# A third of the pair products with samples on partitions, summed along the free axis on ScalarE

## The reference

```python
e = jnp.stack([tbl_0[ids[:, 0]], ..., tbl_39[ids[:, 39]]], axis=1)
vi = x[:, i_idx, :]
vj = x[:, j_idx, :]
viW = jnp.einsum('bpd,pde->bpe', vi, W)
out = jnp.einsum('bpe,bpe->bp', viW, vj)
...
h = jnp.concatenate([z, dense_ctx], axis=1)
h = jnp.maximum(h @ W_top1 + b_top1, 0.0)
h = jnp.maximum(h @ W_top2 + b_top2, 0.0)
y = h @ W_top3
```

## Time and profile before

| | before |
|---|---|
| median of three runs | 1374.25 us |
| the profiled execution's own time | 1374.48 us |
| its span, first to last instruction | 1372.7 us |
| TensorE busy | 1307.9 us, 95% |
| VectorE busy | 928.9 us, 68% |
| GpSimd busy | 604.8 us, 44% |
| ScalarE busy | 83.4 us, 6% |
| mean granted TensorE clock | 0.994 |

### The profile page before, as it was taken

How to read it: one execution, slowest core, us unless ns; L and a number is a source line. 1 busy time by engine, 2 the same in 40 slices (tenths; PEclk the granted TensorE clock), 3 DMA queues, 4 the chain that set the end, 5 groups by cost and what they waited for, 6 DMA issues and landing times.

```text
span 1372.7 us, 17118 instructions
## 1 busy us (share of the span) xinstructions
PE 1307.9 (95%) x7024; PEld 463.4 (34%) x7024; DVE 928.9 (68%) x804; ACT 83.4 (6%) x137; POOL 604.8 (44%) x646
## 2 busy tenths in 40 slices
PE   0699999998999999999999999999999999999998
PEld 0233333332333333333333333333333333333333
DVE  0378877776634788788854588878873478888860
ACT  0000000000000000000000100000000000000001
POOL 6777777777777777754543444451000000000000
PEclk9899999999999999999999999999999999999999
DMA  4233332222222233322211222222110011111100
GB/s 163 42 73 73 70 69 73 73 66 65 65 42 58 66 74 72 74 66 63 65 45 37 47 66 62 62 64 53 47 40 23 23 48 51 50 47 47 32 1 0
DMA packets 49782, 77.38 MB, mean 56 GB/s; under 512 B 13540, under 2 KB 13540, under 8 KB 49576
## 3 DMA queue, kind: packets, MB, share of 16 engines
q1 hardware_dynamic: 29216, 55.26, 13.6%
q0 software_dynamic: 20480, 21.01, 8.4%
q10 hardware_dynamic: 8, 0.01, 0.0%
HBM read 76.22 MB, written 0.01 MB: 56 GB/s over the span
## 4 chain that ended last, share of the span: by engine, by line
PE 86%; POOL 9%; issue 3%; DMA 1%; ACT 1%; POOLq 0%
PE u_ps L311 48%; PE z_ps L328 25%; POOL rows L268 9%; PE turn_ps L342 6%; PE turn_ps L294 3%; PE turn_ps L347 2%; PE u_ps L342 1%; PE u_ps L313 1%; PE u_ps L347 1%; PE turn_ps L351 0%; DMA rows<-in_tbl,ids_all 0%; ACT h_sb L418 0%; DMA ids_all<-in_ids 0%; PE u_ps L351 0%; ACT y_row L424 0%
## 5 line engine op out<-in xcount | busy, mean ns | idle before, releaser
L388 DVE TENSOR_TENSOR prod<-u_ps,x 128x1024 f32<-128x1024 f32 x800 | 928.2, 1218 | 401.8 <-PE u_ps L313 398.4
L313 PE MATMUL u_ps<-x,w_ring 64*128 64x512 f32 x1600 | 759.9, 610 | 0.0
L311 PE MATMUL u_ps<-x,w_ring 64*128 64x512 f32 x1600 | 759.9, 610 | 0.0
L268 POOL DMA_INDIRECT rows<-in_tbl,ids_all x640 | 604.1, 944 | 326.9 <-issue 196.1
L311 PEld LDWEIGHTS u_ps<-x,w_ring 64*128 64x128 f32 x1600 | 279.9, 187 | 420.4 <-issue 324.9
L328 PE MATMUL z_ps<-prod,ones 128*32 128x512 f32 x3200 | 393.4, 601 | 0.0
L313 PEld LDWEIGHTS u_ps<-x,w_ring 64*128 64x128 f32 x1600 | 279.8, 187 | 0.0
L328 PEld LDWEIGHTS z_ps<-prod,ones 128*32 128x32 f32 x3200 | 85.6, 109 | 279.7 <-issue 152.4
L294 PE MATMUL turn_ps<-ident,rows 128*128 128x128 f32 x320 | 53.9, 293 | 60.3 <-DMA rows<-in_tbl,ids_all 54.3
L407 ACT COPY x<-turn_ps 128x512 f32<-128x512 f32 x80 | 46.9, 586 | 635.8 <-PE turn_ps L294 635.8
L342 PE MATMUL turn_ps<-z_sb,mlp_sb 128*128 128x512 f32 x182 | 81.5, 599 | 0.8 <-ACT z_sb L412 0.8
(11 more groups left out here) (19 smaller groups left out, 14.7 us busy)
## 6 DMA issues: line engine op xcount, KB each, us to landing
w_ring<-in_w_pair SPq DMA_DIRECT2D x200, 256.0 KB, 2.7
rows<-in_tbl,ids_all POOLq DMA_INDIRECT x640, 2.5
mlp_sb<-in_mlp SPq DMA_DIRECT2D x1, 2308.0 KB, 11.5
ids_all<-in_ids SPq DMA_DIRECT2D x1, 320.0 KB, 3.3
z_sb<-in_dense_t SPq DMA_DIRECT2D x4, 32.0 KB
out_y<-y_row ACTq DMA_DIRECT2D x4, 2.0 KB
```

Of the source, the lines that this page charges most:

```text
L268: nc.gpsimd.indirect_dma_start(rows[:, slot, s, par * DIM:(par + 1) * DIM], None, tables[f], bass.IndirectOffsetOnAxis(ap=ids_all[:, SUB * ...
L311: pe.matmul(u_ps[:, bank, :], w_ring[0:DIM, c % W_SLOTS, cols], x[0:DIM, b % 2, n_even, :], start=True, stop=True)
L313: pe.matmul(u_ps[:, bank + 1, :], w_ring[DIM:P, c % W_SLOTS, cols], x[DIM:P, b % 2, n, :], start=True, stop=True).then_inc(mains_done, 1)
L388: nc.vector.tensor_tensor(prod[:, full % PROD_SLOTS], u_ps[:, bank:bank + 2, :], other, ALU.mult).then_inc(prods_done, 1)
```

## The change

256 of the 780 pairs are computed the other way round. These are the pairs of duos 4 to 19 with the first four duos (`KEEP`), 64 full units of each block. In their place come 64 units of a new kind, `"R"`: (n, s) is duo n with 128 samples, number s of the block's four. The stationary operand is now 128 samples of the duo (64 partitions), and the matrices of eight pairs move, 512 columns. The product has samples on partitions and eight pairs of 64 numbers along the free axis. VectorE multiplies it with the gathered rows of the first four duos as they came, which are now held for a block in `kept`, and writes one of four slots of `rprod`. The sum over d then runs along the free axis: on ScalarE by 16 instructions of 128x64 with an accumulator output, or, for the first 24 of the new units (all in the first block), on VectorE by one `tensor_reduce`. The sums collect in `zb`, samples on partitions; two turns by TensorE per block (`"zr"`) bring them into two chunks of `z_sb`. The others fill five chunks, so the first dense layer has seven as before.

The units of both kinds are interleaved by `block_units`. The number of slots of `rows` falls from 10 to 6, `x` becomes a ring of 28 duos instead of 40, the matrices come through two rings (4 and 3 slots), the sums of a group come three units behind it, 12 duos of the next block are turned in a block instead of 15, and the dense layers are placed by units (`MLP_AT`). The last dense layers wait for their inputs piece by piece.

```diff
-W_SLOTS = 8
-ROW_SLOTS = 10
+KEEP = 4
+KEPT = 2 * KEEP
+GROUP = 4
+X_SLOTS = 28
+WF_SLOTS, WR_SLOTS = 4, 3
+ROW_SLOTS = 6
+U_SLOTS = 3
+FPROD_SLOTS, RPROD_SLOTS = 2 * GROUP, 4
+SUM_LAG = 3
...
+def block_units(b):
+
+    moving = [("R", n, s) for n in range(KEEP, DUOS) for s in range(SUBS[b])]
+    out, f, r = [], 0, 0
+    while f < NF or r < len(moving):
+        reach = DUOS if f >= NF else STANDING[f][1]
+        due = f >= NF or (r < len(moving) and f >= 8 and r * (NF - 20) <= (f - 8) * len(moving)
+                          and moving[r][1] <= reach)
+        if due:
+            out.append(moving[r])
+            r += 1
+        else:
+            out.append(STANDING[f])
+            f += 1
+    return out
...
+def on_vector(u):
+
+    r = R_AT[u]
+    return r < 24
...
-NEXT_DUOS = 15
+EARLY_DUOS = 12
...
+            at.setdefault(max(0, min(first[n] - 2, (29 * n) // 5)), []).append((0, n))
+    else:
+        for n in range(EARLY_DUOS, DUOS):
+            at.setdefault(max(0, min(first[n] - 3, 8 + 7 * (n - EARLY_DUOS))), []).append((b, n))
+    if b + 1 < NB:
+        free = 116 if b == 0 else 70
+        for n in range(EARLY_DUOS):
+            at.setdefault(free + (len(UNITS[b]) - 4 - free) * n // EARLY_DUOS, []).append((b + 1, n))
+    return at
...
-MLP_AT = {1: ("l1", 0), 2: ("l1", 1), 3: ("l1", 2), 4: ("l1", 3), 5: ("l2", 0), 6: ("l2", 1), 8: ("l3", 0)}
+MLP_AT = {3: ("zr", 0), 5: ("zr", 1), 16: ("l1", 0), 22: ("l1", 1), 28: ("l1", 2), 34: ("l1", 3),
+          40: ("l2", 0), 46: ("l2", 1), 52: ("l3", 0)}
...
+                for half in range(2):
+                    on = slice(half * DIM, (half + 1) * DIM)
+                    if kind == "R":
+                        op = pe.matmul(u_ps[:, bank + half, :], x[on, x_slot(b, n), k * P:(k + 1) * P],
+                                       wr_ring[on, c % WR_SLOTS, :], start=True, stop=True)
+                    else:
+                        m = n - 1 if kind == "D" and half == 0 else n
+                        op = pe.matmul(u_ps[:, bank + half, 0:SIZES[b]],
+                                       wf_ring[on, c % WF_SLOTS, f % GROUP * P:(f % GROUP + 1) * P],
+                                       x[on, x_slot(b, m), 0:SIZES[b]], start=True, stop=True)
+                op.then_inc(mains_done, 1)
...
+            def turn_z(b, c):
+                bank = bank_for(("zr", b, c))
+
+                pe.wait_ge(asums_done, sum(u < UNIT0[b + 1] for u in A_SUMS))
+                pe.wait_ge(vsums_done, sum(u < UNIT0[b + 1] for u in V_SUMS))
+                for s in range(SUBS[b]):
+                    op = pe.transpose(bank[:, s * P:(s + 1) * P], zb[:, s, c * P:(c + 1) * P], ident[:])
+                op.then_inc(turned, 1)
...
+                if kind == "R":
+                    r = R_AT[u]
+                    old = R_UNITS[r - RPROD_SLOTS] if r >= RPROD_SLOTS else None
+                    if old in A_AT:
+
+                        dve.wait_ge(asums_done, A_AT[old] + 1)
+                    elif old in V_AT:
+                        dve.wait_ge(vsums_done, V_AT[old] + 1)
+                    nc.vector.tensor_tensor(rprod[:, r % RPROD_SLOTS], u_ps[:, bank:bank + 2, :],
+                                            kept[:, b % 2, k:k + 1, :].to_broadcast([P, 2, KEPT * DIM]),
+                                            ALU.mult).then_inc(prods_done, 1)
...
+            def sum_over_d(u):
+                b, _, n, s = ALL[u]
+                r = R_AT[u]
+                if b and V_AT[u] == sum(v < UNIT0[b] for v in V_SUMS):
+
+                    dve.wait_ge(turned, turn_at["zr", b - 1, ZR - 1] + 1)
+                dve.wait_ge(prods_done, u + 1)
+                at = (n - KEEP) * 2 * KEPT
+                nc.vector.tensor_reduce(zb[:, s, at:at + 2 * KEPT],
+                                        rprod[:, r % RPROD_SLOTS].rearrange("p h (j d) -> p (h j) d", d=DIM),
+                                        AX.X, ALU.add).then_inc(vsums_done, 1)
...
+            def sum_over_d(u):
+                b, _, n, s = ALL[u]
+                slot = R_AT[u] % RPROD_SLOTS
+                act.wait_ge(prods_done, u + 1)
+                at = (n - KEEP) * 2 * KEPT
+                for j in range(2 * KEPT):
+                    one = rprod[:, slot, j // KEPT, j % KEPT * DIM:(j % KEPT + 1) * DIM]
+                    op = nc.scalar.activation(one, one, ACT.Copy, accum_out=zb[:, s, at + j:at + j + 1])
+                op.then_inc(asums_done, 1)
```

More of the change, by code:

```diff
@@ L23, with standing_units @@
 BLOCK = 512
[L24 removed]
 H1, H2 = 512, 256
 M1, M2 = H1 // P, H2 // P
+SIZES = [512, 512, 512, 512]
+NB = len(SIZES)
+STARTS = [sum(SIZES[:b]) for b in range(NB)]
+SUBS = [n // P for n in SIZES]
+KEEP = 4
+KEPT = 2 * KEEP
 GROUP = 4
[L29 to L30 removed]
+X_SLOTS = 28
+WF_SLOTS, WR_SLOTS = 4, 3
+ROW_SLOTS = 6
 U_SLOTS = 3
[L32 to L36 removed]
+FPROD_SLOTS, RPROD_SLOTS = 2 * GROUP, 4
+SUM_LAG = 3
+def standing_units():
+    out = []
     for n in range(DUOS):
@@ L38, in unit_list @@
         if n % 2:
[L39 to L47, removed]
+            out.append(("D", n, n - 1))
+        out += [("F", n, k) for k in range(KEEP if n >= KEEP else 0, n)]
+    return out
+STANDING = standing_units()
+NF = len(STANDING)
+GROUPS = NF // GROUP
+NT = 2 * NF
 Z_TILES = 64
 K_GROUPS = Z_TILES // (2 * GROUP)
-ZK = -(-NT // Z_TILES)
-Z_LAST = NT - Z_TILES * (ZK - 1)
+ZF = -(-NT // Z_TILES)
@@ L52 @@
+Z_LAST = NT - Z_TILES * (ZF - 1)
 DENSE_ROW = 96
-FIRST_UNIT = {n: min(q for q, u in enumerate(UNITS) if u[1] == n) for n in range(1, DUOS)}
-FIRST_UNIT[0] = 0
+R_DUOS = DUOS - KEEP
+R_PAIRS = R_DUOS * 2 * KEPT
+ZR = R_PAIRS // P
+ZK = ZF + ZR
 W1_COLS, W2_COLS = ZK * H1, M1 * H2
+assert NF % GROUP == 0 and R_PAIRS % P == 0
+def block_units(b):
[11 more added lines that the diff above has]
+            f += 1
+    return out
@@ L162, in dlrm_tower @@
+def dlrm_tower(nc, dense_t, ids, tables, mlp_w, w_standing, w_moving, out, N_DENSE):
+    order = work_order()
+    turn_at = {ev: t for t, ev in enumerate(ev for ev in order if ev[0] in ("duo", "zr", "l1", "l2", "l3"))}
     first_tail = turn_at["l1", NB - 1, 0]
+    for at, ev in enumerate(order):
+        if ev[0] == "duo" and DUOS * ev[1] + ev[2] >= X_SLOTS:
+            old = divmod(DUOS * ev[1] + ev[2] - X_SLOTS, DUOS)
+            assert ("unit", old[0], last_use(*old)) in order[:at], ev
@@ L395, in _ @@
+            due = []
+            for what, b, u in order:
+                if what == "unit":
+                    products(u)
+                    if due:
+                        sum_over_d(due.pop())
+                    if u in V_AT:
+                        due.append(u)
+            for u in due:
+                sum_over_d(u)
         @block.scalar
@@ L433, in _ @@
                     duo(b, n)
+                elif what == "unit" and n in A_AT:
+                    sum_over_d(n)
+                elif what == "zr":
+                    move_zr(b, n)
                 elif what == "sum":
```

338 lines of the change are left out of this document (204 added, 134 removed).

## The result

The changed kernel takes 1392.73 us (median of four, 1391.02 to 1394.64) against 1374.35 us before: a ratio of 1.0132 with a 95% interval of 1.0119 to 1.0145, 1.3% slower. The forecast was 1316 us and 4.2% faster, so both the sign and the size were wrong. That the time lies in the stated range is no merit of the working: the range was drawn wide for a sum on ScalarE that costs 0.31 us or more, and it costs 0.24.

A forecast was written before the change was run, and what follows sets the result against it. TensorE was taken as the bound, GpSimd's gathers pacing the first block; blocks of 347.2, twice 314.4 and 300.5 us plus a 37.7 us tail gave 1314.2 us, with 1.8 us outside the span 1316 us; range 1265 to 1560.

The forecast's parts named there:

- the sum: Whole kernel: 347.2 + 2 x (298.9 + 11.5 + 4) + (282.6 + 13.9 + 4) + 37.7 = 1314.2 us of span.
- The wait of TensorE for the turning bank: Dense layers just behind a duo (units 15, 16, 22): up to 3.7 us; 4 us a block taken for both.
- ScalarE's rate: Units 57 to 186: ScalarE 178.1 us against TensorE's 166.6, behind by 11.5 us; 13.9 in the last block.
- the way of its lag: ScalarE can lag some three new units; then VectorE waits for a slot, three units later TensorE; some 40 us of VectorE waits.
- 736 c + 8.8: ScalarE's time in units 57 to 186: 46 new units of 16 sums, plus 15 copies; 178.1 us at c = 0.23.
- c: Cost of one 128x64 ScalarE sum with accumulator, in a row of such: 0.23 us, range 73 to 371 ns.
- The first block: Paced by GpSimd's gathers; 32 duos needed instead of 35, so it ends at 347 us, 23.5 earlier than 370.7.
- TensorE's own time: TensorE alone: 28.0 us less per block, so 298.9 us for the second and third block, 282.6 for the last.
- the fourth rival: VectorE becomes the bound; if only where new units come in pairs, 5 us a block: 1336 us; within the 0.65 chance.
- The second rival: ScalarE binds, accumulator fetch prevents overlap: 0.314 us a sum, 1544 us; chance 0.22 (c to about 0.34).
- break-even of 0.254: The sum cost c, in us, at which the forecast change neither gains nor loses.
- The chance of 0.33 for slower: Whole kernel: slower 0.33, against faster 0.65 and same 0.02; second way 0.22, third (c = 0.371, 1730 us) 0.11.

## Why the prediction was wrong, step by step

The span came out 75.7 us above the 1314.2 of the sum.

**The wait of TensorE for the turning bank is the step that failed.** The prediction has the right mechanism: "Where a dense layer wants the one turning bank just behind a duo ... TensorE waits for up to one unit's sums, 3.7 us; I take 4 us a block for both." The first half of a block lost 20.7 us, not 4, and the run with later sums gave all of it back. Three things were missed. A copy stands behind two units' sums and the product before them, not one (7.7 us of L614 in the chain). It happens at four places in the first half of a block, also before the second and third dense layers, where I looked only at units 15, 16 and 22. And TensorE came back from its idle time at the lower clock, which made a layer of 6.2 us one of 8.9. Over three blocks that is 50 us more than forecast, two thirds of the error.

**ScalarE's rate was costed about right, the way of its lag wrong.** For units 57 to 186 the sum said 736 c + 8.8; at the measured 0.239 that is 184.7 us, and ScalarE was busy in all of the 179 us between the two copies. The excess over TensorE was 13.2 us, of which 6.9 melt at the block's end, where I had carried nothing over: 6.3 net against 11.5 forecast, 5 us too much per block. The sum let the lag reach TensorE through the four slots: "after that VectorE waits for a slot, and three units later TensorE", some 40 us of such waits in all. The changed kernel has none. Copies stand in the same queue, and they meet the lag first: TensorE waited 23.7 us for copies of the bank of sums, 7.9 of them in this half of the second block. The prediction had these copies in ScalarE's load, but no wait for them. The waits for slots came only with the sums moved behind the copies, 44 us of them. That slack does not carry from the first half to the second held: ScalarE had 46 us of idle time in the first and was the bound in the second.

**The first block** came 20.2 us late: 9.7 for VectorE's reductions and 9.4 for ScalarE's sums by the two runs without them (367.4, 358.0, 348.2), and 1.0 for the rest. (The forecast's terms, 325.41 and 21.3, make 346.7; it went on with 347.2.) I had called the stretch to 186 us one "under waits for gathers" and put unit 76 at 153 us; ScalarE's first sum, of that unit, began at 186.3. I had set TensorE and the gathers side by side and left VectorE out, whose products and reductions of those units filled it.

**TensorE's own time.** Without ScalarE's sums a middle block took 304 us and not 299, and the last 298.6 and not 282.6. Of the last 16 us 3.2 are four more duos, at 0.79 each, that the new table turns in it behind the mark (8 against 4), which I overlooked. The 5 us of every block are what the fourth rival gave VectorE's grip. The longer waits of weight loads for VectorE, 22 us more in the third block and 27 in the last, point that way, but no run shows that they are the loss; the 5 us and some 8 more of the last block stay open. The tail was 2.7 us shorter.

The blocks add up: 20.2 + 2 x 16.6 (5 + 16.7 - 5.1 each) + 25.0 (16 and 9 for ScalarE) - 2.7 = 75.7 us.

**What held**: a new unit's two products cost what the old ones did (TensorE's records 617 ns against 621 for the old kind in the same kernel, VectorE's product 1218 ns, 1216); 2176 records of sums and 115 us less of them (forecast 4 x 29.6 = 118); the gathers' pace for the first block without the rest; c to 4%; VectorE not the bound outside the first block. The second rival put the loss on overlap in ScalarE's pair of instructions, which there is: 0.239 and not 0.314. With c under its break-even of 0.254 the kernel lost all the same, by a way that had no rival of its own, only a term. The chance of 0.33 for slower stood on dearer sums, so it did not foresee this either.

## What to carry to other kernels

When work is given to an idle engine, cost its queue and not only its rate: list what that engine already does for others (here copies that free the one turning bank and the one bank of sums, 6% of its time), and ask how long each of those now waits. Here the same 3712 sums cost 90 us in the order that follows the data and 31 us with the short copies ahead of them. Count all places where an engine hands over such a resource, take the wait as the whole backlog that its slots allow, and add what an idle TensorE loses in clock after it. And when an engine is relieved in a stretch that another paces, read what the third does there.

## What the runs showed of the hardware

- A sum along the free axis on ScalarE is two instructions, an ACTIVATE of 244 ns and a read of the accumulator of 191 ns (medians), which overlap: 0.239 us for each pair of 64 columns. A reduction of 128x1024 to 128x16 on VectorE takes 1.21 us, what ScalarE does in 3.83.
- After an idle time of 5.35 us at the turning bank 14 records of the first dense layer took 8.86 us instead of 6.22. The granted clock was 0.50 from 391 to 395 us, so TensorE ran at its lower level, 1.2 GHz, for part of that layer; over that half of the block it was 0.96, against 1.00 with the later sums.
